# A three-layer transformer kernel on one core: nine waits narrowed, one block in place of two, and the second key chunk loaded ahead of the last value stores

## The chip, the core and the metric

The kernel runs on one core of a Trainium2 chip, as one launch. The metric is the device time of that launch in microseconds (us), as a median over runs. A core has five engines with a queue of instructions each: TensorE (PE, matrix products; PEld is its weight load), VectorE (DVE), ScalarE (ACT), GpSimd (POOL) and SyncE (SP, which here issues nearly all transfers). They meet at semaphores: an instruction raises one, and another engine's queue stands until it has a certain value.

## What is computed

```python
def reference(x, ctx_1024, mask, ...):            # x (2,512,512), ctx (2,8192,512)
    x = x + cross_attention(layernorm(x), ctx, ctx, mask)     # 16 heads of 32, 8192 keys
    x = x + window_attention(layernorm(x))                    # 7 keys, latent keys and values
    x = x + moe_ffn(layernorm(x))     # 16 experts, each takes its best 128 of 1024 tokens
    return x                          # (and a shared FFN for every token)
```

The projections of the context and the experts' products are taken in three terms (high times high, high times low, low times high, each a full pass of PE), the other products in plain fp32.

## The kernel before

The work runs in three stages, each bound together by an order written out by hand on every engine.

**Projection.** The 32 chunks of 512 context rows (16 per batch) are turned into keys and values. For a chunk PE makes four key products (PSUM banks 0 to 3) and four value products (banks 4 to 7) of twelve matmuls each; ACT writes the high part of the keys (`KH`), DVE the low part (`KL`) and the values (`VS`), and SP stores them to `kh_d`, `kl_d` and `v_d`. Ahead of the loop, beside chunk 0, lies the start: the first layernorm, eight groups of four transposes of `XN` that share PSUM banks 4 and 5 in turn (`PS[:, 4 + i % 2]`, line 830) and that ACT copies out (line 754), then eight query products (banks 6 and 7), for which ACT writes `QH` and its square `QQ`, DVE writes `QL` (line 681) and PE sums the squares (`norms`, line 808). On DVE the split of context chunk 1 (`split(1, 1)`, line 626) stands ahead of the first `QL`. Query product n waits for `QL` of product n-2, since they share a bank. After the last chunk DVE computes a flag (`bound`), a bound on the scores. If it holds, the exact maximum (`exact_max_*`) is skipped; with these inputs it is skipped. PE, DVE and SP each read the flag into a register and branch.

**Attention.** For 8 groups of heads and batch, 64 key tiles each: PE makes four score products per tile (`score`, line 421, a ring of six banks, 0 to 5), ACT takes the exponential into one of six buffers `PR` (lines 499, 503), PE multiplies by the values (`values`, line 432, bank 7) and DVE adds the tiles up for the denominators (lines 530, 534). Seven scores run ahead. `KS` (keys) and `VC` (values) are double buffers; SP fills them with `load_keys` (4 transfers) and `load_values` (1). Before the first exponential, ACT waits for every store of keys and values to land (`s_kvst`), DVE and SP too, and POOL sets two constant parts of `KS1` and `QS1` only after that; SP loads the keys of chunk 1 only after POOL. At the end come the output projections `wo0` to `wo3`.

**Middle and experts.** A second `nc.Block()` holds the rest (lines 1177 on). In it four PSUM banks (0 to 3) are handed round by a list, `ORDER`: product number i of the list goes to bank i % 4, `claim` waits until the one four places before it in the list has been evicted, `filled` waits for the product, and `evicted` for its copy out. PE makes `wo4` to `wo7`, turns the four normalised tiles `t20` to `t23` (line 1267), waits until ACT has copied all four out (line 1516), and begins the key product `k00` (line 1274). Window attention, second layernorm and shared FFN follow; there the down products `dn0`, `dn1` (line 1363) stand ahead of the transposes `t34` to `t37`, after which PE waits for their copies and makes the gate logits (line 1339). The experts are 64 steps of gate, up and down products, each with 12 matmuls (lines 1022, 1060). Every step takes three weight tiles of 1 MB, which SP loads into six `RAW` buffers and ACT and DVE split into high and low (lines 924, 929). Before the first gate product PE waits until `dn5`, `dn6` and `dn7` are evicted. In each down product the terms go `HTH*hi, HTH*lo, HTL*hi` four times, after a wait for `HTL` (DVE, line 1143), which needs `HTH` (ACT, line 1103).

## Time and profile before

| | |
|---|---|
| time, median of 3 runs | 2816.34 us (2814.86 to 2817.19) |
| time of the profiled execution | 2814.52 us |
| its span in the profile | 2812.7 us |
| PE busy | 2778.2 us, 99% |
| DVE busy | 2170.9 us, 77% |
| ACT busy | 1722.5 us, 61% |
| granted PE clock, mean | 0.998 of full speed |

A timeline row gives the start in us from the span's start, the duration in us, the engine, the line of the kernel, the instruction, the tile written and the tiles read, the number of instructions merged in the row, and in brackets the idle time of the engine before them with the instruction that ended it. A row of the windows gives for a stretch the busy time of each engine with the number of its instructions, the granted clock of PE as a share of full speed, and the share and rate of the transfers.

### The profile page before, as it was taken

What the parts mean: (1) busy time and instruction counts of PE and PEld (TensorE: products, weight loads), DVE (VectorE), ACT (ScalarE), POOL (GpSimd) and SP (SyncE); (2) the same over time, 40 slices, a digit from 0 to 9 for tenths busy, and PEclk for the clock granted to TensorE, in tenths of its full rate; (3) what the DMA queues carried; (4) which work ended last, traced back from release to release, by engine and by line L of the source; (5) the groups of instructions that cost most, each with busy time, mean ns of one, the idle gap of its engine ahead of it and who ended that gap; (6) DMA issues with size and microseconds to landing.
All of it is one profiled execution on the core that took longest, in us unless ns stands there. A gap on an engine that the chain in (4) does not pass through costs nothing. (4 is left out here: it accounts for less than half of the span.)

```text
span 2812.7 us, 37416 instructions
## 1 busy us (share of the span) xinstructions
PE 2778.2 (99%) x14157; PEld 1766.3 (63%) x14157; DVE 2170.9 (77%) x1600; ACT 1722.5 (61%) x2489; POOL 88.1 (3%) x43
## 2 busy tenths in 40 slices
PE   8999999999999999999999999999999999999998
PEld 5888888888644444444444444445544688888886
DVE  5544444444599999999999999856647898888986
ACT  4222122211499999999999999624621577677775
POOL 0000000000000000000000000000000400000000
PEclk9999999999999999999999999999999999999999
DMA  5555555555655555555555555321130699999995
GB/s 219 199 193 197 191 188 200 188 200 182 189 132 137 132 137 133 136 133 136 144 125 144 125 144 126 77 73 46 46 127 19 265 372 350 348 344 350 342 348 197
DMA packets 229104, 515.51 MB, mean 183 GB/s; under 512 B 18130, under 2 KB 84050, under 8 KB 199628
## 3 DMA queue, kind: packets, MB, share of 16 engines
q1 hardware_dynamic: 225372, 505.15, 56.8%
q0 software_dynamic: 3584, 8.39, 1.3%
q8 instruction: 92, 1.51, 0.2%
q14 instruction: 56, 0.46, 0.1%
HBM read 400.03 MB, written 113.44 MB: 183 GB/s over the span
## 5 line engine op out<-in xcount | busy, mean ns | idle before, releaser
L534 DVE TENSOR_TENSOR AC<-AC,PR 128x2048 f32<-128x2048 f32 x448 | 988.4, 2281 | 5.0 <-ACT PR L499 5.0
L499 ACT ACTIVATE PR<-PS 128x512 f32<-128x512 f32 x1024 | 567.6, 610 | 55.5 <-PE PS L421 43.2
L421 PEld LDWEIGHTS PS<-QS,KS 128*128 128x128 f32 x2048 | 364.9, 188 | 336.3 <-ACT PR L503 181.3
L421 PE MATMUL PS<-QS,KS 128*128 128x512 f32 x2048 | 563.7, 416 | 4.1 <-ACT PR L499 3.1
L503 ACT ACTIVATE PR<-PS 128x1024 f32<-128x1024 f32 x512 | 502.4, 1051 | 0.0
L432 PE MATMUL PS<-PR,VC 128*32 128x512 f32 x4096 | 493.3, 599 | 0.7 <-ACT PR L499 0.7
L929 DVE TENSOR_TENSOR WL<-RAW,WH 128x2048 fp32r<-128x2048 f32 x192 | 436.3, 2286 | 58.4 <-ACT WH L924 58.4
L736 ACT ACTIVATE KH<-PS,bk_s 128x512 fp32r<-128x512 f32 x128 | 88.3, 690 | 536.5 <-PE PS L792 536.2
L924 ACT ACTIVATE WH<-RAW 128x2048 fp32r<-128x2048 f32 x192 | 362.0, 1912 | 7.5 <-PE PS L1363 5.2
L631 DVE SCALAR_TENSOR_TENSOR KL<-PS,bk_s,KH 128x512 fp32r<-128x512 f32 x128 | 95.5, 749 | 258.5 <-ACT KH L736 258.5
L432 PEld LDWEIGHTS PS<-PR,VC 128*32 128x32 f32 x4096 | 106.9, 109 | 217.5 <-issue 172.3
L1022 PE MATMUL PS<-WL,XEH 128*128 128x512 f32 x512 | 200.5, 392 | 0.0
L1022 PE MATMUL PS<-WH,XEL 128*128 128x512 f32 x512 | 200.1, 391 | 0.0
L1022 PE MATMUL PS<-WH,XEH 128*128 128x512 f32 x512 | 199.6, 390 | 0.0
L800 PE MATMUL PS<-WVH,CH 128*128 128x512 f32 x512 | 199.4, 389 | 0.0
L800 PE MATMUL PS<-WVH,CL 128*128 128x512 f32 x512 | 199.2, 389 | 0.0
L800 PE MATMUL PS<-WVL,CH 128*128 128x512 f32 x512 | 199.2, 389 | 0.0
L792 PE MATMUL PS<-CH,WKH 128*128 128x512 f32 x496 | 192.9, 389 | 0.0
L792 PE MATMUL PS<-CL,WKH 128*128 128x512 f32 x496 | 192.9, 389 | 0.0
L792 PE MATMUL PS<-CH,WKL 128*128 128x512 f32 x496 | 192.9, 389 | 0.0
L640 DVE TENSOR_TENSOR VS<-PS,bv_s 128x512 f32<-128x512 f32 x128 | 85.1, 686 | 103.0 <-PE PS L800 103.0
L1103 ACT ACTIVATE HTH<-PS 128x512 fp32r<-128x512 f32 x64 | 38.3, 599 | 148.6 <-PE PS L1044 148.6
(208 smaller groups left out, 3210.7 us busy)
## 6 DMA issues: line engine op xcount, KB each, us to landing
KS<-kh_d SPq DMA_DIRECT2D x256, 256.0 KB
RAW<-in_gw SPq DMA_DIRECT2D x64, 1024.0 KB, 5.4
RAW<-in_up_w SPq DMA_DIRECT2D x64, 1024.0 KB, 5.4
RAW<-in_down_w SPq DMA_DIRECT2D x64, 1024.0 KB, 5.4
kh_d<-KH SPq DMA_DIRECT2D x32, 1024.0 KB, 4.4
kl_d<-KL SPq DMA_DIRECT2D x32, 1024.0 KB, 6.5
v_d<-VS SPq DMA_DIRECT2D x128, 256.0 KB, 2.9
KS<-kl_d SPq DMA_DIRECT2D x128, 256.0 KB
```

The lines of the kernel that those rows point to most:

```text
L421: pe.matmul(PS[:, m % RING, :], KS[N % 2][:, j, t * P:(t + 1) * P], QS[bg % 2][:, j, :], start=True, stop=True).then_inc(s_s, 1)
L432: m = pe.matmul(PS[j * DH:(j + 1) * DH, OUTB, :], VC[N % 2][:, t, j * DH:(j + 1) * DH], PR[tile % BUFS][:, j, :], start=q == 0, stop=q == ...
L499: nc.scalar.activation(PR[tile % BUFS][:, 2 * hp + jj], PS[:, bank + jj, :], ACT.Exp, scale=SCALE).then_inc(s_exp, 1)
L503: nc.scalar.activation(PR[tile % BUFS][:, 2 * hp:2 * hp + 2], PS[:, bank:bank + 2, :], ACT.Exp, scale=SCALE).then_inc(s_exp, 2)
L534: v.tensor_tensor(a[i % 2][:], a[i % 2][:], p[:], ALU.add).then_inc(s_acc, 1)
L631: v.scalar_tensor_tensor(KL[s][:, g, :], PS[:, g, :], bk_s[:, g:g + 1], KH[s][:, g, :].bitcast(F32), ALU.add, ALU.subtract).then_inc(s_kl, 1)
L736: nc.scalar.activation(KH[s][:, g, :], PS[:, g, :], ACT.Identity, bias=bk_s[:, g:g + 1]).then_inc(s_kh, 1)
L792: mm = pe.matmul(PS[:, g, :], w[:, c, g * P:(g + 1) * P], a[s][:, c, :], start=(k == 0), stop=(k == len(terms) - 1))
L800: mm = pe.matmul(PS[:, G + t, :], a[s][:, c, t * P:(t + 1) * P], w[:, c, :], start=(k == 0), stop=(k == len(terms) - 1))
L924: nc.scalar.activation(WH[n % PAIRS][:], RAW[:, n % RAWS], ACT.Copy).then_inc(s_hi, 1)
L929: nc.vector.tensor_tensor(WL3[n % PAIRS][:], RAW[:, n % RAWS], WH[n % PAIRS][:].bitcast(F32), ALU.subtract).then_inc(s_lo, 1)
L1022: m = pe.matmul(PS[:, bank, :], x[e % 2][:, c, :], w[:, c, :], start=False, stop=i == len(terms) - 1)
```

## The change

The parts, in the order of the run:

1. **Start.** The transposes go round three banks (4, 5, 6), so that number i waits for the copy of i-3, not i-2. The query products swap banks (7, then 6), and product 1 waits for the copy of transpose 5. DVE's split of chunk 1 moves behind the second `QL`. The last `norms` moves behind the first value product.
2. **Into the attention.** PE waits for the flag and reads it before the ninth of the last twelve value matmuls. Scores 0 to 3 no longer wait for all values to be evicted, only for the last `KL` (`s_kl`); scores 4 and 5 wait for the value bank that they overwrite; all values are waited for after score 6. ACT waits for the last value matmul, the last `VS` and the query stores, not for the key and value stores; it takes a one-column exponential (`EXP1`) after its last `KH`, which brings the table load there. DVE waits for the stores only at head group 1, SP at key chunk 2. POOL sets its two constants once all key products are done. SP issues the four key loads of chunk 1 ahead of the four last value stores, after waits for POOL's constants (`s_row`, 4) and for chunk 1's stores.
3. **Out of the attention.** The second block is gone: its bodies are functions that follow on each engine; SP waits for the last normalised output (`s_norm`, 8), POOL for `s_row`. `wo7` moves behind `t23`.
4. **Second normalisation's end.** `dn1` moves behind `t37`.
5. **Into the experts.** The wait for `dn5`, `dn6`, `dn7` becomes one for each bank's last user, ahead of the product that overwrites it.
6. **Last step.** The last down product takes its eight `HTH` terms first, after a wait for `HTH`, and waits for `HTL` only ahead of the last four.

`EXP1` is 4 bytes a partition behind `bq_s`; every other buffer keeps its address.

```diff
-        ORDER = ([f"wo{i}" for i in range(TT)] + [f"t2{i}" for i in range(4)]
+        ORDER = ([f"wo{i}" for i in range(TT - 1)] + [f"t2{i}" for i in range(4)] + ["wo7"]
...
-                 + [f"pj{i}" for i in range(4, TT)] + ["g07", "u07", "dn0", "dn1"] + [f"t3{i}" for i in range(4, TT)] + ["gate1", "dn2", "dn3"]
+                 + [f"pj{i}" for i in range(4, TT)] + ["g07", "u07", "dn0"] + [f"t3{i}" for i in range(4, TT)] + ["dn1", "gate1", "dn2", "dn3"]
...
         def attention_sync(sp):
-            for s in range(2):
-                sp.wait_ge(s_kvst[s], STORES * NC_ALL // 2 + 1)
-            sp.dma_start(WO[:], wo).then_inc(s_wo, 16)
-            sp.wait_ge(s_row, 4)
             for N in range(1, BG * NCH):
                 bg, n = divmod(N, NCH)
+                if N == 2:
+                    for s in range(2):
+                        sp.wait_ge(s_kvst[s], STORES * NC_ALL // 2 + 1)
+                    sp.dma_start(WO[:], wo).then_inc(s_wo, 16)
...
-                load_keys(sp, N % 2, N, bg % B * NCH + n)
+                if N >= 2:
+                    load_keys(sp, N % 2, N, bg % B * NCH + n)
                 if N >= 2:
                     sp.wait_ge(s_pv, (N - 1) * KT)
+                else:
+                    sp.wait_ge(s_vps, 2 * KT + NC_ALL * KT)
                 load_values(sp, N % 2, N)
         def attention_gpsimd(pool):
-            for s in range(2):
-                pool.wait_ge(s_kvst[s], STORES * NC_ALL // 2 + 1)
-            pool.wait_ge(s_vps, 2 * KT + NC_ALL * KT)
+            pool.wait_ge(s_kps, NC_ALL * G)
...
                 if m >= RING:
                     pe.wait_ge(s_exp, exponentials(m - RING))
+                elif m >= G:
+                    pe.wait_ge(s_vs, NC_ALL * KT + m - G + 1)
...
             for m in range(LEAD):
                 score(m)
+            pe.wait_ge(s_vs, (NC_ALL + 1) * KT)
...  (attention_scalar)
-            for s in range(2):
-                act.wait_ge(s_kvst[s], STORES * NC_ALL // 2 + 1)
+            act.wait_ge(s_vps, 2 * KT + NC_ALL * KT)
+            act.wait_ge(s_vs, (NC_ALL + 1) * KT)
+            for i in range(2):
+                act.wait_ge(s_qst[i], 32 * (BG // 2))
...
                 sp.dma_start(kl_d[:, n].rearrange("g p k -> p g k"), KL[s][:].bitcast(F32)).then_inc(s_kvst[s], 16)
+                sp.wait_ge(s_row, 4)
+                sp.wait_ge(s_kvst[1], STORES + 1)
+                load_keys(sp, 1, 1, 1)
                 for t in range(KT):
...
-                split(1, 1)
                 for n in range(BG):
                     g = n % G
+                    if n == 2:
+                        split(1, 1)
...
-                    if i >= 2:
-                        pe.wait_ge(s_xt, i - 1)
+                    if i >= 3:
+                        pe.wait_ge(s_xt, i - 2)
                     for c in range(DC):
-                        m = pe.transpose(PS[:, 4 + i % 2, c * P:(c + 1) * P], XN[:, i, c * P:(c + 1) * P], ident[:])
+                        m = pe.transpose(PS[:, 4 + i % 3, c * P:(c + 1) * P], XN[:, i, c * P:(c + 1) * P], ident[:])
...
-                norms(BG - 1)
                 pe.wait_ge(s_wlo, 2)
                 for t in range(KT):
+                    if t == 1:
+                        norms(BG - 1)
...
-                values(n, s, 3)
-                pe.wait_ge(s_b, FLAG)
-                exact_max_tensor(pe)
-                pe.wait_ge(s_vs, (NC_ALL + 1) * KT)
+                bounded = values(n, s, 3, flagged=True)
+                pe.wait_ge(s_kl, (NC_ALL + 1) * G)
+                exact_max_tensor(pe, bounded)
                 attention_tensor(pe)
+                middle_tensor(pe)
...  (middle, PE)
-                for i in range(4, TT):
+                for i in range(4, TT - 1):
                     output_projection(pe, i)
                 for i in range(4):
                     turn(2, i)
+                output_projection(pe, TT - 1)
...  (experts, PE)
             pe.wait_ge(s_bs, 5)
-            for name in ("dn5", "dn6", "dn7"):
-                evicted(pe, name)
             gate(0)
```

The order of the instructions as built shows two of the places. SyncE between the last chunk's key stores and the second key chunk of the attention (`KS`: keys, `VC`: values), before (the branch with the exact maximum is left out):

```order
L610 DMA kl_d<-KL 128x4x512
L613 DMA v_d<-VS 128x4x128 x4
L310 TENSOR_LOAD flag
...
L388 DMA WO<-in_wo 128x2048
L152 DMA KS<-kh_d 32x4x512
L152 DMA KS<-kl_d 32x4x512
L152 DMA KS<-kh_d 32x4x512
L155 DMA KS<-mask_d 1x4x512
L160 DMA VC<-v_d 128x512
```

And in the change:

```order
L1609 DMA kl_d<-KL 128x4x512
L152 DMA KS<-kh_d 32x4x512
L152 DMA KS<-kl_d 32x4x512
L152 DMA KS<-kh_d 32x4x512
L155 DMA KS<-mask_d 1x4x512
L1615 DMA v_d<-VS 128x4x128 x4
L312 TENSOR_LOAD flag
...
L160 DMA VC<-v_d 128x512
L393 DMA WO<-in_wo 128x2048
```

The four key transfers stand ahead of the value stores now, and the output weights behind the values of chunk 1. TensorE at the end of the attention (`WO<-AT`: output projections, `ident,EX`: the transposes `t20` to `t23`, `XT,WK`: `k00`), before:

```order
L252 MATMUL PS<-WO,AT 128x512 x8
L439 MATMUL PS<-AC,ones 32x512 x8
L252 MATMUL PS<-WO,AT 128x512 x8
L542 UNCONDITIONAL_BRANCH
L1259 UNCONDITIONAL_BRANCH
L252 MATMUL PS<-WO,AT 128x512 x16
L1267 MATMUL PS<-ident,EX 128x128 x16
L1274 MATMUL PS<-XT,WK 128x512 x8
```

And in the change:

```order
L254 MATMUL PS<-WO,AT 128x512 x8
L444 MATMUL PS<-AC,ones 32x512 x8
L254 MATMUL PS<-WO,AT 128x512 x20
L943 MATMUL PS<-ident,EX 128x128 x16
L254 MATMUL PS<-WO,AT 128x512 x4
L950 MATMUL PS<-XT,WK 128x512 x8
```

The two branches between the blocks are gone, and four matmuls, `wo7`, stand between the transposes and `k00`.

## Rows read from the trace of the kernel before

**Rows 1.** The page, part 1: busy time by engine, share of the span, instructions.

```profile
PE 2778.2 (99%) x14157; PEld 1766.3 (63%) x14157; DVE 2170.9 (77%) x1600; ACT 1722.5 (61%) x2489; POOL 88.1 (3%) x43
```

**Rows 2.** Windows: the attention stage, then the expert stage.

```profile
760.00:1820.00 1060.00, 1059.31 (x6508) 482.14 (x6501) 1047.84 (x478) 993.53 (x1530) 0.00 (x0) 1.00 0.55 132
2250.00:2790.00 540.00, 540.00 (x2516) 446.08 (x2515) 481.78 (x322) 386.84 (x306) 50.27 (x15) 1.00 0.95 345
```

**Rows 3.** Timeline of the start, 22 to 62 us: PE, then DVE; last, one window.

```profile
22.40 1.18 PE L830 MATMUL PS<-ident,XN 128*128 128x128 f32 x8 [0.55 <-ACT KL L754]
23.87 1.18 PE L830 MATMUL PS<-ident,XN 128*128 128x128 f32 x8 [0.29 <-ACT KL L754]
...
34.63 1.95 PE L840 MATMUL PS<-VS,WO 128*128 128x512 f32 x4 [1.00 <-issue]
...
58.04 0.50 PE L808 MATMUL PS<-QQ,BLR 128*128 128x512 f32 x1 [1.21 <-ACT QQ L769]
...
31.59 2.27 DVE L626 TENSOR_TENSOR CL<-AT,CH 128x2048 fp32r<-128x2048 f32 x1
33.79 1.39 DVE L681 SCALAR_TENSOR_TENSOR QL<-PS,bq_s,QH 128x512 fp32r<-128x512 f32 x2
...
22.00:24.00 2.00, 1.30 (x9) 1.00 (x10) 2.00 (x6) 1.74 (x7) 0.00 (x0) 1.00 0.99 373
```

**Rows 4.** Timeline into the attention, 734 to 760 us: PE, ACT, POOL, DVE; last, one window.

```profile
744.04 0.39 PE L800 MATMUL PS<-WVH,CL 128*128 128x512 f32 x1
745.28 1.65 PE L421 MATMUL PS<-QS,KS 128*128 128x512 f32 x6 [0.85 <-DVE VS L640]
750.07 4.82 PE L421 MATMUL PS<-QS,KS 128*128 128x512 f32 x9 [3.14 <-ACT PR L499]
754.83 2.70 PE L432 MATMUL PS<-PR,VC 128*32 128x512 f32 x16
757.46 2.18 PE L421 MATMUL PS<-QS,KS 128*128 128x512 f32 x8
759.57 1.92 PE L432 MATMUL PS<-PR,VC 128*32 128x512 f32 x16
...
748.13 1.28 ACT L499 ACT_TABLE_LOAD   x1 [14.26 <-DMA v_d<-VS]
...
748.18 1.80 POOL L407 MEMSET KS<- 32x2048 f32 x1 [747.73 <-DMA v_d<-VS]
...
734.57 2.28 DVE L635 TENSOR_REDUCE kmax<-KH 128x4 f32<-128x2048 f32 x1
...
749.40:756.60 7.20, 6.40 (x21) 3.05 (x25) 2.29 (x1) 7.19 (x12) 2.32 (x2) 0.53 0.85 258
```

**Rows 5.** Timeline out of the attention, 1818 to 1845 us: PE, then DVE.

```profile
1818.90 7.13 PE L252 MATMUL PS<-WO,AT 128*128 128x512 f32 x16
1827.23 13.97 PE L252 MATMUL PS<-WO,AT 128*128 128x512 f32 x32 [1.19 <-DVE X L1659]
...
1843.99 7.10 PE L1274 MATMUL PS<-XT,WK 128*128 128x512 f32 x16 [1.04 <-ACT XT L1516]
...
1826.39 0.69 DVE L1659 TENSOR_TENSOR X<-X,PS 128x512 f32<-128x512 f32 x1 [3.27 <-PEq L542]
...
1833.92 1.91 DVE L1684 TENSOR_SCALAR EX<-X,ln_tmp 128x512 f32<-128x512 f32 x4
```

**Rows 6.** Timeline of PE around the gate logits, 2102 to 2110 us.

```profile
2102.94 1.91 PE L1267 MATMUL PS<-ident,EX 128*128 128x128 f32 x16
2105.90 3.59 PE L1339 MATMUL PS<-AT,GW 128*16 128x512 f32 x8 [1.04 <-ACT AT L1516]
```

**Rows 7.** Timeline of PE at the first expert product, 2208 us.

```profile
2208.40 0.47 PE L1011 MATMUL PS<-BIAS,PICK 128*128 128x512 f32 x1 [0.98 <-DVE X L1755]
```

**Rows 8.** Timeline of the last down product, 2799 to 2804 us: PE, then DVE.

```profile
2801.00 0.47 PE L1060 MATMUL PS<-WH,HTH 128*128 128x512 f32 x1 [1.50 <-DVE HTL L1143]
...
2800.16 0.69 DVE L1143 TENSOR_TENSOR HTL<-PS,HTH 128x512 fp32r<-128x512 f32 x1 [3.04 <-ACT HTH L1103]
```

More of the change, by code:

```diff
@@ new lines, in program @@
+        XEH, XEL = ([se(f"{n}{i}", [P, DC, CAP], F32R) for i in range(2)] for n in ("XEH", "XEL"))
+        for i in range(4, PAIRS):
+            weight_pair(i)
+        GE, HE = ([se(f"{n}{i}", [CAP, 512]) for i in range(2)] for n in ("GE", "HE"))
+        HTH, HTL = ([se(f"{n}{i}", [P, FT, CAP], F32R) for i in range(2)] for n in ("HTH", "HTL"))
+        YO = [se(f"YO{i}", [CAP, D]) for i in range(2)]
+        s_g1, s_ga, s_gb = sem("second_gathered"), sem("tokens_gathered"), sem("last_tokens_gathered")
@@ new lines, in experts_scalar, with silu, hidden_hi, rows_hi @@
+        def experts_scalar(act):
+            def silu(S):
+                act.wait_ge(s_used, NTH["g", S] + 1)
+                if S >= 2:
+                    act.wait_ge(s_hid, S - 1)
+                nc.scalar.activation(GE[S % 2][:], PS[:, S % 2, :], ACT.Silu).then_inc(s_si, 1)
+            def hidden_hi(S):
+                act.wait_ge(s_t, S + 1)
+                if S >= 2:
+                    act.wait_ge(s_used, NTH["d", S - 2] + 1)
+                nc.scalar.activation(HTH[S % 2][:], PS[:, 4, :].rearrange("p (f t) -> p f t", f=FT), ACT.Copy).then_inc(s_hth, 1)
+            def rows_hi(e):
+                act.wait_ge(s_xrt, e)
+                if e >= 2:
+                    act.wait_ge(s_used, NTH["u", (e - 1) * FC - 1] + 1)
+                nc.scalar.activation(XEH[e % 2][:], PS[:, 7, :].rearrange("p (c t) -> p c t", c=DC), ACT.Copy).then_inc(s_xh, 1)
+            def split(n):
+                if EARLY <= n < len(TILES):
+                    weights_hi(act, n)
+            for n in range(EARLY, 4):
+                split(n)
+            filled(act, "dn7")
+            for n in range(4, PAIRS):
+                split(n)
+            silu(0)
+            for S in range(STEPS):
+                if S % FC == 2 and S // FC + 1 < E:
+                    rows_hi(S // FC + 1)
+                split(3 * S + PAIRS)
+                hidden_hi(S)
+                split(3 * S + PAIRS + 1)
+                if S + 1 < STEPS:
+                    silu(S + 1)
+                split(3 * S + PAIRS + 2)
@@ new lines, in experts_vector, with hidden, hidden_lo, rows_lo @@
+        def experts_vector(dve):
+            v = nc.vector
+            def hidden(S):
+                dve.wait_ge(s_si, S + 1)
+                dve.wait_ge(s_used, NTH["u", S] + 1)
+                if S >= 2:
+                    dve.wait_ge(s_t, S - 1)
+                v.tensor_tensor(HE[S % 2][:], PS[:, 2 + S % 2, :], GE[S % 2][:], ALU.mult).then_inc(s_hid, 1)
+            def hidden_lo(S):
+                dve.wait_ge(s_hth, S + 1)
+                v.tensor_tensor(HTL[S % 2][:], PS[:, 4, :].rearrange("p (f t) -> p f t", f=FT), HTH[S % 2][:].bitcast(F32),
+                                ALU.subtract).then_inc(s_htl, 1)
+            def rows_lo(e):
+                dve.wait_ge(s_xh, e + 1)
+                v.tensor_tensor(XEL[e % 2][:], PS[:, 7, :].rearrange("p (c t) -> p c t", c=DC), XEH[e % 2][:].bitcast(F32),
+                                ALU.subtract).then_inc(s_xl, 1)
+            def output(e):
+                dve.wait_ge(s_used, NTH["d", e * FC + FC - 1] + 1)
+                if e >= 2:
+                    dve.wait_ge(s_sc, 16 * (e - 1))
+                v.tensor_scalar(YO[e % 2][:], PS[:, 5 + e % 2, :], score[:, e:e + 1], None, ALU.mult).then_inc(s_y, 1)
+            def split(n):
+                if EARLY <= n < len(TILES):
+                    weights_lo(dve, n)
+            for n in range(EARLY, PAIRS):
+                split(n)
+            hidden(0)
+            for S in range(STEPS):
+                if S % FC == 0 and S:
+                    output(S // FC - 1)
+                if S % FC == 2 and S // FC + 1 < E:
+                    rows_lo(S // FC + 1)
+                split(3 * S + PAIRS)
+                hidden_lo(S)
+                split(3 * S + PAIRS + 1)
+                if S + 1 < STEPS:
+                    hidden(S + 1)
+                split(3 * S + PAIRS + 2)
+            output(E - 1)
@@ L1868, in by_contraction @@
+                middle_gpsimd(pool)
 def by_contraction(w):
```

1724 lines of the change are left out of this document (832 added, 892 removed).

## The prediction

> **What bounds the kernel now.** I read the page's first part first: PE is busy for 99% of the span, DVE for 77% [rows 1]. Then the windows by stage. In the attention PE is busy for 1059.31 of 1060 us and DVE for 1047.84; in the experts PE is busy all 540 us [rows 2]. So the bodies are full, the change alters no instruction in them, and it can only win the stops between them. I therefore looked through PE's timeline for rows with an idle time in brackets near each edited place, and then at the engine named there. A stop of PE counts in full where PE is busy without a break from there to the next edited place, since everything behind it then starts earlier by the same time.
>
> One reading rule: an idle time counts from the modelled end of the last matmul, and matmuls that follow one another overlap. The last value matmul lasts 0.39 us [rows 4], but a score or product of one pass starts 0.23 us behind the one before (a term of twelve takes 2.7 us). A stop that vanishes thus gives back its idle time and about 0.17 us of that tail.
>
> **Part 1, the start.** PE stops three times between the groups of transposes, 0.55, 0.29 and once more 0.28 us, each time for ACT's copy out of the bank used two transposes ago (two of the three stand in [rows 3]). With a third bank the copy of three ago is wanted, which has been done for one copy longer; the stops go: 1.1 us. The third query product starts at 34.63 after 1.00 us of idle, named "issue". The code has it wait for the first `QL`, and DVE starts that at 33.79, behind the split of chunk 1 that began at 31.59 and took 2.27 us [rows 3]. With the split two `QL` later, the first `QL` is early by those 2.3 us, PE does not stop: 1.0 us. What is late next is the split: it has until the keys of chunk 1, more than 30 us on, so nothing waits. The last `norms` stops PE for 1.21 us on ACT's square [rows 3]; behind a value product of twelve matmuls (2.7 us) the square is ready: 1.2 us. Sum 3.3 us. Bounds: 2.2, if the transposes still pace on ACT, and 3.8, with a tail of 0.17 at three places.
>
> **Part 2, into the attention.** Today ACT waits until 748.13 for the last value store, then loads its table for 1.28 us, so the first exponential starts at about 749.4 [rows 4]. POOL starts its constants at 748.18, also after the stores. In the change the last wait of ACT is for the last `VS`. PE's first score starts at 745.28 today, released by that same copy of DVE [rows 4], so the copy ends at 745.2. The table was loaded at about 734, behind the last `KH`, where ACT has 14.26 us of idle ahead of it. Scores 0 and 1 need to be done as well; between the last value matmul (start 744.04, next slot 744.27) and 745.28 lie 1.0 us in which PE now reads the flag and branches, so 1.0 us is an upper bound for both. The branch stays there, ahead of `VS`. The read moves in front of the last four value matmuls, and what it stops PE for delays the last `VS` by as much: between 0 and 1.0 us. I take 0.3, since the flag is ready by then and the read shares those 1.0 us with the branch. The first exponential then starts at 745.6, not 749.4: **3.8 us**, between 3.1 and 4.1.
>
> The Trainium skill ("ScalarE: Activation LUTs", What ACT_TABLE_LOAD costs) gives a table switch 1.28 us and a drain of 1.38 more, so moving it would be worth 2.7 us and the part 5.2. The trace does not agree: the load starts at 748.13 and PE, which waits for the first exponential (some 0.6 us), goes on at 750.07, which leaves no room for a drain behind the load [rows 4].
>
> The stop has a second price. PE stands for 3.14 us and the granted clock falls to 0.53 of full speed over 749.4 to 756.6, that is to 1.2 GHz for nearly all of it [rows 4]. The first 16 value products take 2.70 us against 1.92 later: 0.8 us lost. The three scores ahead of them that no longer wait for an exponential start some 0.2 us further apart each: 0.6 us. In the change PE works off and on from 744.9 (six scores, then one or two per exponential, no pause over 1 us). At the start the grant stayed at 1.00 from 22 to 24 us although PE was busy for only 1.30 of those 2.00 us [rows 3], so I expect it to stay here: **1.4 us** more, bounds 0 and 1.4.
>
> Keys of chunk 1: SP now waits for POOL (two fills of 1.80 us from about 733), issues four transfers in some 2 us, and is at the value stores at about 739, some 0.6 us later than now; the last store waits for `VS` at 745.2 in any case, so it lands when it did. Its readers are now SP for chunk 2 and DVE at head group 1, 130 us later. The keys are wanted at score 16, about 8 us after the first exponential; they land by about 743. Values of chunk 1 go out at about 746. `WO` goes out at 748.2 as today, chunk 2's keys after score 16: nothing late.
>
> **Part 3, out of the attention.** DVE starts to add `wo0` at 1826.39, after 3.27 us of idle that ends with the block, though its own last work ended at 1823.1 [rows 5]. PE therefore waits 1.19 us for the first bank before `wo4`. Without the block DVE starts at 1823.1: the stop goes. PE also waits 1.04 us until ACT has copied the four transposes, before `k00` at 1843.99 [rows 5]; `wo7`, 3.45 us of matmuls (a quarter of 13.8), now lies there. The transposes need `XN6`, which DVE ends at 1835.8 today, from 1833.92 on; it starts 3.2 us earlier, and the transposes 4.7 (1.4 for the stop, 3.4 for `wo7`), so they fall at about 1836.4 with `XN6` ready at 1832.6. They hold. Sum with two tails: **2.6 us**, bounds 2.2 and 2.7. What is late next is DVE's second normalisation: `wo7`, its last input, comes last now, so it ends some 3 us later than today when measured from `k00`; the latent keys that it would hold up come 7 us behind `k00`, by then it is done.
>
> **Parts 4 and 5.** PE waits 1.04 us for ACT's copies before the gate logits [rows 6]; `dn1`, 6.9 us, lies there now: **1.2 us** with the tail. Before the first gate product PE waits 0.98 us for DVE's last sum, `dn7` [rows 7]. Its bank (3) is wanted only by the second up product, 9 us later; the first gate product's bank was freed long before: **1.15 us**. The raw weights come no earlier, so ACT and DVE have 1.15 us less in hand; transfers were busy for 0.95 of the expert stage, yet PE was never idle in it [rows 2].
>
> **Part 6.** PE waits until 2801.00 for `HTL`, which DVE starts at 2800.16, as soon as `HTH` is there [rows 8]. Eight `HTH` terms are 1.8 us, more than the 0.69 us of DVE. PE starts at about 2800.3: **0.7 us**.
>
> **Sum:** 3.3 + 3.8 + 1.4 + 2.6 + 1.2 + 1.15 + 0.7 = 14.2 us (rounded). The profiled execution took 2814.5 us, so it would be 2800.3; the median of the runs is 1.8 us above it, which gives 2816.3 - 14.2 = **2802.1 us**.
>
> **The rivals.** *The clock falls all the same* (0.24). PE has little work for about 4 us beside the first exponentials, and it may count as idle. For it: the clock did fall after one stop of 3.1 us. Against: no such stop is left. Gain 12.8, time 2803.5.
>
> *New stops at the flag* (0.13). The read of the flag holds PE for its full 1.0 us, or POOL's fills, now at about 733 to 737, hold up DVE's `kmax` (2.28 us from 734.57 [rows 4]), from which the flag comes. The trace has never both at once; by rows the price lies between 0 and the two fills, 3.6 us. I put the case at 1 to 3.6 us, time 2803 to 2806. The Trainium skill ("SBUF — State Buffer", SBUF: two separate sides) has GpSimd and VectorE take a shared pair of ports as an exclusive lock, but for VectorE only in a two-port mode or with two SBUF inputs against a GpSimd read; a fill reads nothing, so by the page this costs 0. No run shows it yet.
>
> *Part 2 does nothing* (0.06). ACT may stand on something else that lands as late, or chunk 1's early keys delay the value stores and SP. Gain 9.0, time 2807.3. Against: the wait list of ACT then has only PE, DVE and stores of the start.
>
> *The body locks into another phase* (0.07). PE, ACT and DVE meet 256 times in a cycle of two tiles (1060 us, 4.1 us each) on rings of six; started from another offset, with keys a chunk further ahead, a cycle may be longer. From 14.2/256 = 0.055 us per cycle, 1.3%, it eats the whole gain; with 2% it costs 21 us and the time is 2823. Against: PE and DVE are full [rows 2] and addresses and instructions are the same. 0.04 of the chance is for a result within the bound, 0.03 for slower.
>
> **How the numbers follow.** Forecast 0.50 at 2802.1, then 0.24, 0.13, 0.06, 0.07. A measurement of this kernel tells about 0.2%, 5.6 us, from no change. All but the last case lie beyond it: faster 0.93, same 0.04, slower 0.03. The upper bounds of the terms give 15.6 us, and the runs before spread by 1.2 us about their median: low end 2799.4. The high end takes in the clock's case, most of the flag's, and part 2 without effect: 2807.4. The last case and the tails are left out.
>
> **What would show it.** Right: no idle between the transposes; the first value product near 55 us; the first exponential 1.2 to 1.6 us after the last value matmul; a grant of 1.00 there and the second batch of value products at 1.9 us; `k00` directly behind `wo7`; no idle before the gate logits and the first gate product; the last down product 0.7 us nearer to its transposes. Wrong: an attention stage longer than 1065 us from the first exponential to the last value product, a pause inside the last twelve value matmuls, or new DMA waits of ACT in the first 40 us of the experts.

## The result and the profile after

| | before | changed |
|---|---|---|
| median (lowest to highest), 6 runs each | 2816.98 us (2814.86 to 2820.08) | 2802.57 us (2800.69 to 2806.19) |
| ratio, with its 95% interval | | 0.9951 (0.9938 to 0.9964) |
| time of the profiled execution | 2814.52 us | 2801.63 us |
| its span | 2812.7 us | 2799.8 us |
| PE busy | 2778.2 us | 2775.1 us |
| granted PE clock, mean | 0.998 | 0.999 |

The time lies 0.5 us from the forecast and within the range. The medians differ by 14.4 us, the spans by 12.9 us. The trace shows where they come from, and that the close match rests in part on errors that cancel.

The start, timeline of PE and of DVE in the changed kernel (columns as in [rows 3]):

```profile
19.91 4.37 PE L1842 MATMUL PS<-ident,XN 128*128 128x128 f32 x32 [0.21 <-DVE XN L125]
24.12 1.88 PE L1854 MATMUL PS<-VS,WO 128*128 128x512 f32 x4
...
31.22 1.88 PE L1854 MATMUL PS<-VS,WO 128*128 128x512 f32 x4
...
53.19 0.39 PE L1811 MATMUL PS<-WVH,CH 128*128 128x512 f32 x1
...
30.22 0.73 DVE L1685 SCALAR_TENSOR_TENSOR QL<-PS,bq_s,QH 128x512 fp32r<-128x512 f32 x1
...
33.24 2.28 DVE L1629 TENSOR_TENSOR CL<-AT,CH 128x2048 fp32r<-128x2048 f32 x1
```

The 32 transposes are one row without a stop, `QL` starts at 30.22 ahead of the split, and none of the idle times of [rows 3] is left. PE waits 0.21 us for the first `XN` instead. Into the attention, PE, then ACT, POOL and DVE, and one window:

```profile
738.15 0.39 PE L1811 MATMUL PS<-WVL,CH 128*128 128x512 f32 x1
738.65 0.47 PE L1811 MATMUL PS<-WVH,CL 128*128 128x512 f32 x1
...
739.42 0.40 PE L1811 MATMUL PS<-WVH,CL 128*128 128x512 f32 x1
739.66 2.75 PE L426 MATMUL PS<-QS,KS 128*128 128x512 f32 x8
742.75 0.73 PE L426 MATMUL PS<-QS,KS 128*128 128x512 f32 x2 [0.35 <-ACT PR L511]
...
745.56 1.93 PE L437 MATMUL PS<-PR,VC 128*32 128x512 f32 x16
747.42 2.17 PE L426 MATMUL PS<-QS,KS 128*128 128x512 f32 x8
...
740.70 1.09 ACT L507 ACTIVATE PR<-PS 128x512 f32<-128x512 f32 x2 [10.28 <-DVE VS L1643]
...
728.24 1.81 POOL L410 MEMSET KS<- 32x2048 f32 x1 [727.79 <-PE PS L1799]
...
729.60 2.28 DVE L1638 TENSOR_REDUCE kmax<-KH 128x4 f32<-128x2048 f32 x1
...
740.70:747.90 7.20, 6.43 (x30) 2.45 (x29) 2.29 (x1) 7.20 (x11) 0.00 (x0) 1.00 0.81 244
```

The first exponential starts 1.28 us behind the start of the last value matmul (739.42); in [rows 4] it was 5.38 us. The grant stays at 1.00, and the first batch of value products takes 1.93 us, not 2.70. The gap from 738.15 to 738.65 (0.50 where 0.23 is the rule) is the read of the flag: 0.27 us. DVE's `kmax` takes 2.28 us beside POOL's fill, as it did alone [rows 4].

Out of the attention the projections run from `wo2` to `wo6` in one row, without the stops of [rows 5], and `wo7` stands behind the transposes, with `k00` directly behind it at 1831.29:

```profile
1808.84 17.43 PE L254 MATMUL PS<-WO,AT 128*128 128x512 f32 x40
1826.11 1.91 PE L943 MATMUL PS<-ident,EX 128*128 128x128 f32 x16
1827.86 3.60 PE L254 MATMUL PS<-WO,AT 128*128 128x512 f32 x8
```

And then what the prediction did not have. Timeline of PE in the experts, of the changed kernel:

```profile
2193.64 0.40 PE L693 MATMUL PS<-WH,XEH 128*128 128x512 f32 x1
...
2226.86 0.47 PE L740 MATMUL PS<-WH,HTH 128*128 128x512 f32 x1 [2.01 <-DVE HTL L821]
...
2787.57 0.47 PE L740 MATMUL PS<-WH,HTH 128*128 128x512 f32 x1 [0.78 <-ACT HTH L781]
```

The idle time ahead of the first product [rows 7] and half of that ahead of the last down product [rows 8] are gone, as is the one of [rows 6] ahead of the gate logits. The first expert product comes 15.06 us earlier than before, but 33 us on PE stops for 2.01 us. ACT's queue says why. The waits of ACT in the 65 us from 2185 us on, which begin 9 us ahead of the first expert product (who waited for whom, us in total, times, longest), changed kernel:

```profile
ACT WH L595 <- DMA RAW<-in_gw: 4.5, 3, 2.1
ACT WH L595 <- DMA RAW<-in_down_w: 1.7, 2, 1.4
ACT WH L595 <- DMA RAW<-in_up_w: 1.5, 2, 0.9
```

The same view of the kernel before, from 2200 us on:

```profile
ACT WH L924 <- DMA RAW<-in_gw: 1.4, 3, 0.6
...
ACT WH L924 <- DMA RAW<-in_down_w: 0.5, 1, 0.5
ACT WH L924 <- DMA RAW<-in_up_w: 0.4, 1, 0.4
```

7.7 us of waiting for weights against 2.3. ACT copies the raw weights in order; while it stands for one that has not landed, the `HTH` behind it waits. And DVE takes the low part of the same weight ahead of `HTL`. DVE, changed kernel:

```profile
2223.82 2.29 DVE L600 TENSOR_TENSOR WL<-RAW,WH 128x2048 fp32r<-128x2048 f32 x1 [1.65 <-ACT WH L595]
2226.03 0.68 DVE L821 TENSOR_TENSOR HTL<-PS,HTH 128x512 fp32r<-128x512 f32 x1
```

`HTH` is done at 2224.27 (ACT's row of it stands further down), but `HTL` starts only at 2226.03, behind this split, and PE's down product at 2226.86 behind `HTL`. So a gate weight that PE needs only for a later step holds up the down product through two queues.

The account of the two profiled spans, each part as the change of a distance between two PE instructions, so that what happened ahead of it does not enter:

| part | distance | before, us | changed, us | gain | forecast |
|---|---|---|---|---|---|
| loads at the start | span start to first transpose | 20.82 | 19.91 | 0.91 | 0 |
| 1 | first transpose to last value matmul, without the read | 723.22 | 719.24 | 3.98 | 3.3 |
| 2, read of the flag | in the last value group | 0 | 0.27 | -0.27 | -0.3 |
| 2, first exponential | from the last value matmul | 5.38 | 1.28 | 4.10 | 4.1 |
| 2, clock | from there to the second score batch | 8.04 | 6.72 | 1.32 | 1.4 |
| attention | second score batch to last sum product | 1059.59 | 1059.57 | 0.02 | 0 |
| 3 | last sum product to `k00` | 26.94 | 24.30 | 2.64 | 2.6 |
| 4 | `k00` to the gate logits | 261.91 | 260.76 | 1.15 | 1.2 |
| 5 | gate logits to first expert product | 102.80 | 101.59 | 1.21 | 1.15 |
| late weights | third to fourth group of hidden transposes | 9.08 | 11.39 | -2.31 | 0 |
| 6 | last transposes to last down product | 2.10 | 1.37 | 0.73 | 0.7 |
| end | last down product to span end | 11.70 | 12.23 | -0.53 | 0 |

With the rounding these make the 12.9 us. The forecast of the exponential is 3.8 net of the read. A score batch is the stretch of scores between two batches of value products; the second is the row at 747.42 above (757.46 in [rows 4]).

### The profile page after: what moved, and what is told of

The parts are those of the page before. It is cut to its first block, busy times and chain, and to the rows that moved or that the text cites. A ratio compares the mean times of both kernels' runs of the same rounds, so it can differ in the third digit from the quotient of the medians.

```text
span 2799.8 us, 37407 instructions
## 1 busy us (share of the span) xinstructions
PE 2775.1 (99%) x14157; PEld 1765.3 (63%) x14157; DVE 2171.2 (78%) x1600; ACT 1722.0 (62%) x2490; POOL 88.4 (3%) x43
## 4 chain that ended last, share of the span: by engine, by line
PE 97%; DVE 1%; DMA 1%; issue 0%; ACT 0%; SPq 0%; POOL 0%; DVEq 0%; ACTq 0%
PE PS L426 19%; PE PS L437 17%; PE PS L1811 12%; PE PS L1799 12%; PE PS L693 12%; PE PS L950 7%; PE PS L740 6%; PE PS L1039 2%; PE PS L444 1%; PE PS L682 1%; PE PS L254 1%; PE PS L1008 1%; PE PS L1854 1%; PE PS L719 1%; DMA RAW<-in_gw 1%; PE PS L973 1%
## 5 line engine op out<-in xcount | busy, mean ns | idle before, releaser
L595 ACT ACTIVATE WH<-RAW 128x2048 fp32r<-128x2048 f32 x192 | 362.2, 1914 | 12.9 <-PE PS L1039 5.2
```

The source lines that it names most:

```text
L595: nc.scalar.activation(WH[n % PAIRS][:], RAW[:, n % RAWS], ACT.Copy).then_inc(s_hi, 1)
```

## The experiments

Milestones below are distances like those of the table, from one profiled execution of each kernel; where nothing differs most of them repeat to 0.05 us (the attention body to 0.6). Medians, where given, are over 5 to 7 executions; four kernels ran once. All kernels are edits of the changed one. Parts 2 and 5 were taken apart in this way; for parts 1, 3, 4 and 6 there are the rows and distances above, and no kernel that undoes them.

**Part 5 against late and early weights.** First PE's old wait alone:

```diff
             pe.wait_ge(s_bs, 5)
+            for name in ("dn5", "dn6", "dn7"):
+                evicted(pe, name)
             gate(0)
```

> TensorE again waits for dn5, dn6 and dn7 to be evicted before the first gate product (part 5 undone, all else as in the change). Theory A (the experts' start is paced by the weight loads): the 1.2 us come back before the first gate product, but TensorE's pause ahead of a down product some 30 us on, 2.0 us in the change, shrinks to 0.8 to 1.0 us, so the span stays at 2799.8 within 0.5 us. Rival B (the pause is a chance of that one execution): TensorE waits 1 us at the gate and not at the down product, as in the kernel before, and the span from the first gate product on is 2.3 us shorter than in the change. Rival C (part 5 is worth its whole price): span +1.2 us, the later pause unchanged.

Second, three loads ahead of the last store:

```diff
             for i in range(4, TT):
+                if i == TT - 1:
+                    load_raw(sp, RAWS)
+                    load_raw(sp, RAWS + 1)
+                    load_raw(sp, RAWS + 2)
                 evicted(sp, f"dn{i}")
...
-            for n in range(RAWS, len(TILES)):
+            for n in range(RAWS + 3, len(TILES)):
```

> SyncE issues the experts' weight loads 6, 7 and 8 ahead of its wait for dn7 and the last store of the base output, instead of behind it. Theory A: the pause of 2.0 us ahead of the down product near 2227 us goes, because these loads start some 3.4 us or more earlier; span 2.3 to 2.4 us shorter, about 2797.4. Rival D (the engines of the transfers are full there, gathers and loads share them, and the issue time does not matter): the pause stays at 1.5 to 2.0 us or moves to another weight, span within 0.5 us of 2799.8.

Third, both edits:

> Both edits of the two kernels before: TensorE waits for dn5 to dn7 and loads 6 to 8 are issued ahead of the last store. Theory A: no pause at the down product, 1 us of pause before the first gate product, so 1.2 us longer than with the loads ahead alone, about 2798.6. Under theory A part 5 is worth 0 with late loads and 1.2 us with early ones. Rival D: equal to the kernel with the wait alone.

| | gate logits to first expert product | third to fourth hidden transposes | gate logits to the fourth |
|---|---|---|---|
| before | 102.80 | 9.08 | 139.48 |
| changed | 101.59 | 11.39 | 140.60 |
| wait kept | 102.95 | 9.09 | 139.62 |
| loads ahead | 101.58 | 9.09 | 138.29 |
| both | 102.92 | 9.10 | 139.60 |

With late loads part 5 wins 1.36 us at the gate and loses 2.30 behind it: this stage is 1.0 us **longer** than with the wait kept. With the loads ahead part 5 is worth 1.31 us. Theory A is right that late weights pace this stretch; its size was off, since the pause vanished wholly with the wait kept, where I had expected 0.8 to 1.0 us. Taken alone, the kernel with the wait kept fits rival B, chance, just as well: 1 us at the gate, no pause behind it, 2.3 us shorter from there. What rules B out is that the pause came in every one of the eight profiled executions with part 5 and late loads (below), and in none of the six others. SyncE's rows show the lever. Changed kernel:

```profile
2177.35 17.30 SPq L919 DMA_DIRECT2D out<-X  x4
2194.70 0.43 SPq L588 DMA_DIRECT2D RAW<-in_up_w  x1
```

With the loads ahead:

```profile
2179.46 12.19 SPq L923 DMA_DIRECT2D out<-X  x3
2191.69 0.43 SPq L588 DMA_DIRECT2D RAW<-in_up_w  x1
```

The first of these loads waited behind `dn7`'s store, not for its buffer. The whole middle runs 2.1 us later in this execution; counted from the gate logits or the first expert product the load goes out 5.1 us earlier. ACT then has no wait for a weight in the same 65 us. Rival D falls, and a window shows why. The same 9 us in both kernels, counted from the gate logits, first the changed kernel, then the loads ahead (the last two columns are the share and the rate of the transfers in GB/s):

```profile
2191.00:2200.00 9.00, 9.00 (x35) 6.39 (x35) 6.43 (x6) 4.33 (x3) 6.62 (x6) 1.00 0.82 263
```

```profile
2193.10:2202.10 9.00, 9.00 (x36) 6.40 (x35) 6.44 (x6) 4.32 (x3) 5.41 (x4) 1.00 1.02 420
```

The transfers are full from about 2200 us on in the changed kernel, but not ahead of it; the early loads use that room. The medians, 2803.56 (wait kept), 2801.43 (loads ahead) and 2803.14 us (both), do not contradict it; the first two spans are equal (2799.6 and 2799.7) because the second execution lost 1.6 us between `k00` and the gate logits, where its grant was 0.83 from 1870 to 1880 us. The third lost 6.3 us there (span 2806.9). So neither span is the one that was expected (2797.4 and 2798.6), and the reading rests on the distances.

**Part 2 undone**, all its edits at once:

> The whole of part 2 undone (stores waited for by ACT, POOL and SyncE as before, no early table load, late read of the flag, scores behind all values, chunk 1's keys behind the value stores), all else as in the change. My theory: the first exponential comes about 9 to 10 us after the start of the last value matmul... that is 5.4 us after the matmul against 1.3; the granted clock falls to about 0.5 again; the second batch of value products starts 5.4 us later, of which 4.1 is the stop and 1.3 the clock; total 5.4 us longer, span about 2805.2, ratio to before 0.997. Rival (part of what I put down to part 2 was won by the start's different phase): less than 4 us.

Measured: first exponential 5.40 us behind the last value matmul, second score batch 13.40 us (before 13.42, changed 8.00). Median 2807.95 us (2807.64 to 2811.77), ratio to before 0.997 (0.9959 to 0.9982). That is 5.4 us over the changed kernel's first median and 3.9 over that of all its 17 executions, so the median alone doesn't settle the size; the distance does. The part is worth what its rows say; the other theory falls. In one thing the kernel is not as before: its wait for the last `VS` stands ahead of the branch, and its first score comes 1.71 us behind the last value matmul, not 1.24. The first exponential waits for the stores either way.

**What in part 2 does it.** Four kernels: the table load not brought forward, ACT waiting for the stores, both, and the flag read late.

```diff
-                nc.scalar.activation(EXP1[:], ones[:, 0:1], ACT.Exp)
```

> The one-column exponential behind the last key eviction is left out (a value that nothing reads), so ScalarE loads its table behind the wait for the last value eviction. By the row of the kernel before (load 1.28 us, exponential right behind it) the first exponential comes 1.28 us later against the last value matmul, 2.56 instead of 1.28 us behind it, and the second batch of value products 1.3 us later. By the Trainium skill (ScalarE: Activation LUTs, What ACT_TABLE_LOAD costs) it would be 2.66 us. TensorE has one pause of some 1.6 us there. Clock: theory 1 (a pause as long as the 3.1 us of before is needed): stays at 1.00, second batch 8.0 + 1.3 = 9.3 us behind the last value matmul; theory 2 (any longer pause there does it): falls, 0.8 to 1.3 us more.

```diff
-            act.wait_ge(s_vps, 2 * KT + NC_ALL * KT)
-            act.wait_ge(s_vs, (NC_ALL + 1) * KT)
+            for s in range(2):
+                act.wait_ge(s_kvst[s], STORES * NC_ALL // 2 + 1)
```

> ScalarE waits for all key and value stores again before its first exponential, the table load stays early. The last value store lands about 2.9 us behind the last value eviction, so the first exponential comes 2.9 us later than in the change, about 4.2 us behind the last value matmul; TensorE's pause is 2.0 to 2.5 us. Theory 1: the clock stays, second batch 8.0 + 2.9 = 10.9 us behind the last value matmul. Theory 2: it falls, second batch 11.7 to 12.2 us behind.

> Both: ScalarE waits for the stores and loads its table behind that wait, as in the kernel before; everything else of part 2 is as in the change. First exponential 4.2 us later than in the change, 5.4 us behind the last value matmul. The clock falls by both theories, so the second batch comes 4.2 + 1.3 = 5.5 us later than in the change. That is the whole of part 2: the other edits (scores' waits, flag, POOL, SyncE's order) would be worth nothing beside it. Rival: the eight free first scores keep the clock up, second batch only 4.2 us later.

```diff
-                bounded = values(n, s, 3, flagged=True)
+                values(n, s, 3)
+                pe.wait_ge(s_b, FLAG)
+                bounded = pe.value_load(flag[0:1, 0:1])
```

> TensorE reads the flag behind the last value matmul instead of ahead of the ninth of the last twelve. My term: the read in the middle delays the last value eviction by 0.27 us in the change. So here no pause in the last twelve, the last value matmul 0.27 us earlier, and the first exponential 0.27 us earlier too, if the read and the branch (0.3 to 1.0 us) are over before TensorE is wanted; the first score starts 0.5 to 1.2 us behind the last value matmul instead of 0.24. Rival: ScalarE then waits for the first two scores, not for the eviction, and the first exponential is 0 to 0.5 us later: the early read is worth up to 0.5 us.

| kernel | PE's longest idle time between the first scores | first exponential behind last value matmul | second score batch behind it | grant behind the pause |
|---|---|---|---|---|
| changed | 0.35 | 1.28 | 8.00 | 1.00 |
| table load late | 1.42 | 2.56 | 9.28 | 1.00 |
| ACT waits for stores | 3.76 | 4.90 | 12.94 | 0.50 |
| both | 5.05 | 6.15 | 13.53 | 0.50 |
| part 2 undone | 2.72 | 5.40 | 13.40 | 0.50 |
| flag read late | 0.36 | 1.27 | 7.99 | 1.00 |

The four took 2804.54, 2811.00, 2807.70 and 2803.81 us, each in the one execution; with the dips of the clock elsewhere these times tell less than the distances. The table load costs its own 1.28 us and no more. ACT, with the late table load:

```profile
740.49 1.28 ACT L507 ACT_TABLE_LOAD   x1 [11.83 <-DVE VS L1643]
741.79 1.09 ACT L507 ACTIVATE PR<-PS 128x512 f32<-128x512 f32 x2
```

The Trainium skill ("ScalarE: Activation LUTs", What ACT_TABLE_LOAD costs) would have 1.38 us of drain more; the trace does not agree. Nor does it where ACT comes from work: in the changed kernel the load starts at 728.92, 0.02 us behind the last `KH`, and `EXP1` follows at 730.21. The wait for the stores costs 3.62 us, 0.7 more than I had expected, and with it the clock falls. One window of the same place in the kernel with the late table load and in the one that waits for the stores (the grant is the third column from the right):

```profile
743.90:751.10 7.20, 7.02 (x39) 3.13 (x43) 3.72 (x2) 7.14 (x12) 0.00 (x0) 1.00 0.58 199
```

```profile
743.90:751.10 7.20, 6.44 (x21) 3.01 (x25) 2.29 (x1) 7.15 (x11) 0.00 (x0) 0.53 0.45 159
```

So a pause of 1.42 us did not lower the clock here, and theory 2 falls. Theory 1 is borne out only in part: the kernel that waits for the stores paused for 3.76 us, not for the 2.0 to 2.5 that were to test it, and with part 2 undone a pause of 2.72 us, with one of 1.32 us 4 us ahead of it, was enough. The two waits of ACT make up the whole of part 2. With both restored the second score batch came 5.53 us later, 5.5 expected, but that match is luck: the exponential came 4.87 us later, not 4.2, and the clock cost 0.66 us, not 1.3, since PE stood through part of the slow stretch. The rival with the free scores falls, the grant went to 0.50. Beside ACT's old waits all the other edits of part 2, the key loads ahead of the value stores, POOL's earlier fills and the free scores, win nothing (13.53 us with them, 13.40 without). Whether ACT's early start needs them is not tested.

The late read is the surprise. The last value matmul comes 0.34 us earlier than in the changed kernel (685.89 instead of 686.23 us behind the first value product), the first score still 0.23 us behind it:

```profile
740.31 0.39 PE L1811 MATMUL PS<-WVH,CL 128*128 128x512 f32 x1
740.54 0.84 PE L426 MATMUL PS<-QS,KS 128*128 128x512 f32 x3
```

Read and branch cost nothing there. The 1.0 us of [rows 4] were the wait for `VS` alone, and the early read buys nothing and costs 0.3 us. A branch behind the wait may cost something: with part 2 undone, where it stands so, the first score comes 0.47 us later than before (1.71 against 1.24). No kernel changes this alone.

**The change again, beside two better ones.** The changed kernel word for word; then with loads ahead and the late read; then also with the product `v01` of the second attention in two halves (`product` takes the part as its last argument):

```diff
-            product("v01", WV6, XT2[0], 1)
+            product("v01", WV6, XT2[0], 1, range(0, 2))
             slot(0, 0)
+            product("v01", WV6, XT2[0], 1, range(2, DC))
```

> The changed kernel once more, word for word, on the same chip as the two below. If the pause ahead of the down product near 2227 us comes from part 5 and late weight loads, it is there again, between 0.9 and 2.5 us (the six executions with part 5 and late loads so far: 2.3, 0.9, 2.5, 2.5, 1.0, 1.7). If it was chance, it can be 0. Median 2802.5, lowest 2800.5 to 2801.

> The change with loads 6 to 8 ahead of the last store of the base output and the flag read behind the last value matmul. From the runs before: 0.34 us for the flag, 0.9 to 2.5 us for the pause in the experts. So no pause ahead of the down product, no pause in the last twelve value matmuls; median 1.2 to 2.9 us under the changed kernel's of the same job. The dips of the granted clock between 1870 and 1905 us (1.65 us for a short one) stay as likely as before. Rival: only the 0.34 us remain, since another weight is late instead.

> As the kernel before it, and the four matmuls of v01 in the second attention are cut in two: c = 0 and 1 ahead of the window scores 1, c = 2 and 3 behind them. VectorE, idle for 2.1 us ahead of scores 1, gets them 1.7 us earlier; TensorE's pause of 1.33 us ahead of scores 2 goes and later ones move by VectorE's earlier start. 1.0 to 1.8 us shorter from k00 to the gate logits than 260.8 us. Theory P (the pause of 1.33 us starts the dips of the clock): the first dip, seen in 7 of 10 executions, is gone or rare, so the spread of the runs shrinks. Rival Q (it is the small matmuls around it, 32 columns wide): dips as before.

| | median (lowest to highest) | ratio to before, 95% |
|---|---|---|
| changed, again | 2807.85 us (2800.86 to 2808.98) | 0.9965 (0.9954 to 0.9977) |
| loads ahead, late read | 2800.28 us (2799.76 to 2801.52) | 0.9942 (0.9929 to 0.9955) |
| and `v01` halved | 2800.69 us (2798.71 to 2801.66) | 0.9943 (0.993 to 0.9955) |

The pause is there again (11.40 us against 9.08, so 2.32) and is gone in the other two. The change's median is 5.35 us over the 2802.5 that I had expected. The second kernel is quicker than the change by 7.6 us of medians, far more than the 2.6 us that its milestones give; with it goes the clock, whose mean over the execution was 0.997 in four of the change's six and 0.998 or 0.999 in all five of the second kernel's. The halved product takes the pause of 1.33 us away, but the profiled execution had its dip at the next pause (1.22 us) instead. The products and transposes in that dip took 3.3 us more than in the changed kernel; without it the 262.58 us from `k00` to the gate logits would be 259.3 by this estimate, 1.5 under the change's, as expected. By the median it is level with the kernel before it. Theory P is not shown; one execution can't tell how often the dips come.

**A third time**, to see one of the longer executions from inside:

> The changed kernel a third time. Of its 12 executions so far 6 took 2806 to 2809 us at a mean granted clock of 0.997 to 0.998, the others 2800.7 to 2804.0; of 15 executions of the three kernels that have part 5 and the early loads, none took over 2801.7. Theory X: the slow ones lose 5 to 7 us by dips of the clock in the second attention (1870 to 1905 us), as in the profiled execution of the kernel with both edits; then a slow profiled execution here has 265 us or more from k00 to the gate logits, and the difference between the kernels is chance. Theory Y: they lose it by a fall of the clock at the pause of 0.9 to 2.5 us in the experts; then it has over 12 us between the third and the fourth group of hidden transposes, or a grant under 1.00 behind it. If the profiled execution is a quick one, this stays open.

Median 2803.89 us (2801.17 to 2808.78), and the profiled execution was the longest of them: span 2807.0. Both theories hold in it, each for a part. From `k00` to the gate logits it took 265.44 us, 4.68 over 260.76, and between the third and fourth hidden transposes 13.12 us, 1.7 more than the 11.4 of the others; 0.2 of that is the pause (2.24 against 2.01 us), 1.5 the clock. Its windows in the second attention and behind the pause in the experts:

```profile
1870.00:1880.00 10.00, 8.67 (x45) 4.38 (x44) 7.72 (x8) 7.16 (x34) 0.00 (x0) 0.87 0.00 0
1890.00:1900.00 10.00, 9.52 (x39) 5.79 (x40) 8.20 (x18) 5.64 (x26) 0.00 (x0) 0.66 0.15 61
2230.00:2240.00 10.00, 7.76 (x29) 6.10 (x28) 9.64 (x6) 6.23 (x4) 0.00 (x0) 0.83 1.01 422
```

And PE at the pause, with matmuls of 0.63 us where 0.39 is the rule:

```profile
2232.50 0.77 PE L740 MATMUL PS<-WH,HTH 128*128 128x512 f32 x1 [2.24 <-DVE HTL L821]
2233.06 0.63 PE L740 MATMUL PS<-WL,HTH 128*128 128x512 f32 x1
```

4.7 + 1.5 = 6.2 us lost by the clock: that is most of the 7.2 us by which this span exceeds the first one of the change (2799.8).

## Why the prediction was right, and where not

**Part 1** was under-sized. 3.98 us against 3.3, above my upper bound of 3.8. The transposes gave 1.33 (1.1 forecast), the `QL` 1.17 (1.0), and 1.48 came behind, for the last `norms` (1.2). Each stop gives back its tail as well: I had stated that rule, and left it to the bound instead of adding it to the sum here, as I did in part 3. The bound had it for three stops where there are five. The term that was mis-sized is this one, 3.98 measured for 3.3. (The upper bounds of all terms add up to 15.05 us, not to the 15.6 of the prediction, which set the low end 0.6 us too low; the median is not near it.)

**Part 2** held in each term: 4.10 less 0.27 for the exponential (3.8 forecast), 1.32 for the clock (1.4). The experiments show both of ACT's waits and the clock behind them as causes. The step that failed in it is small: I took the flag's read for a share of the 1.0 us behind the last value matmul, and it had no share in them. **Parts 3, 4 and 6** came out within 0.05 us, by distances alone.

**Part 5** is the step that failed. The prediction said: "The raw weights come no earlier, so ACT and DVE have 1.15 us less in hand; transfers were busy for 0.95 of the expert stage, yet PE was never idle in it [rows 2]." The shortage was named and then dismissed by a window that begins at 2250 us, behind the place where it hurts. The rows that would have told are ACT's waits for `RAW` above, 2.3 us in all, and these two of the kernel before, DVE and PE at the same down product:

```profile
2238.59 0.68 DVE L1143 TENSOR_TENSOR HTL<-PS,HTH 128x512 fp32r<-128x512 f32 x1
...
2239.71 0.39 PE L1060 MATMUL PS<-WH,HTH 128*128 128x512 f32 x1
```

`HTL` is ready at 2239.27, 0.44 us ahead of its product. With PE early by 1.2 us that alone is a pause of 0.8. The rest is the transfers' own. SyncE issued the first load behind `dn7`'s store 13.85 us earlier than before (2194.70, 2208.55). The gate weight that holds up this `HTH` is the sixth of them, issued 15.04 us earlier (2202.56, 2217.60); it was there only 12.56 us earlier (2221.87, 2234.43), while the first expert product came 15.06 us earlier. ACT, changed kernel:

```profile
2221.87 1.92 ACT L595 ACTIVATE WH<-RAW 128x2048 fp32r<-128x2048 f32 x1 [2.14 <-DMA RAW<-in_gw]
2223.69 0.58 ACT L781 ACTIVATE HTH<-PS 128x512 fp32r<-128x512 f32 x1
```

The size of the pause follows the landing of this weight. Counted from the gate logits ACT takes it at 128.5 us in the kernel before, at 128.4 and 128.5 in the two executions with the shortest pause (part 2 undone and both of ACT's waits restored: 0.9 and 1.0), at 129.2 with 1.7 us (flag read late) and at 129.8 to 130.0 with 2.3 to 2.5 us. Why the loads took longer on the way in most of them, beside the gathers of the same time, no run separates. Of eight profiled executions with part 5 and the loads as they were (the change three times, five with edits elsewhere), all have it, from 0.9 to 2.5 us without the clock. So part 5 as it stands is worth between +0.3 and -1.3 us, where the prediction had +1.15.

The total came out right because errors cancel: -2.3 for the weights and -0.5 at the end against +0.7 in part 1 and +0.9 of earlier loads at the start, and by the medians, which put before 2.5 us above its profiled execution and the change 0.9. The last two are chance: in the traces of the twelve experiments the first transpose starts at 19.5 to 21.2 us. Over all its 17 timed executions the changed kernel has a median of 2804.0 us, still within the range, and 12 to 13 us under before.

**The rivals.** The clock did not fall at the attention's entry: none of the ten traces with ACT's early start shows the fall of [rows 4]. POOL's fills held up nothing, which is what the Trainium skill ("SBUF — State Buffer", SBUF: two separate sides) gives for a fill that reads nothing; the trace agrees, 2.28 us for `kmax` both times. The body locked into no other phase: 1059.5 to 1060.0 us in all fourteen traces. I had only one rival that spoke of a new wait, and placed it at the flag; "new DMA waits of ACT in the first 40 us of the experts" stood in the list of what would prove me wrong, and that one happened. So did "a pause inside the last twelve value matmuls", 0.27 us of it, which my own term of 0.3 for the read had allowed for; that sign could not have told right from wrong.

## What to carry to other kernels

Before costing an earlier start of a stage as a pure gain, look at the first tens of microseconds behind it: which queue's operands come no earlier, and how much is in hand there; an average over the stage hides it. Then ask what the late operand waits for in its own queue, since moving three issues ahead of one store wait brought back more than narrowing the wait had won. And a pause of PE is to be costed with the clock that may fall behind it: 1.3 us behind the 3.1 us at the attention's entry, and 1.6 us or more in ten of thirteen traces behind one of 1.3 us in the second attention, though whether that pause starts the dip is not shown.

## What the runs showed of the chip that was not expected

- The granted clock dips in the second attention in some executions and not in others. All profiled executions have the same pauses of PE there (1.33 and 1.22 us, between small matmuls). Of the thirteen traces of kernels whose second attention is as in the change or before, three (before, the change's first, wait kept) have no dip, seven a short one, which costs 1.6 us in this stretch, three longer ones, which cost 4.7 to 6.3 us. At the attention's entry a pause of 1.42 us lowered nothing. In the experts a pause of 2.24 us lowered it in the change's third execution, and one of the same 2.24 us did not with the late table load. What decides it stays open.
- It makes most of the spread. Of the 17 executions of the change, 9 took over 2804 us; of the 15 of the three kernels with part 5 and early loads (loads ahead, with the late read, with `v01` halved), none took over 2801.8. The fall behind the experts' pause explains 1.5 us of that; why the longer dips in the second attention, which lies ahead of the edit, were also missing there is not shown. The three kernels were grouped after their times were known: the one with the loads ahead and the wait kept, whose profiled execution has long dips, had two of five over 2804. For 0 of 15 against 9 of 17 chance alone is a poor account, but the runs show no other. So of the 7.6 us between the medians only the 2.6 of the milestones are shown as the edits' work.
- From the last down product to the end of the span all thirteen edited kernels take 12.1 to 12.4 us, before 11.7. The work in it is the same and the last store is issued as far behind the product. There is only one trace of before, so whether its end was short by chance is open; no experiment looked for a cause.
